# x turned over by TensorE, two tiles in every body, and the bias laid into the projection's bank by VectorE

## The reference

```python
qkv = (x @ w_qkv).reshape(b, n, 3, H, hd).transpose(2, 0, 3, 1, 4)
q, k, v = (qkv[0], qkv[1], qkv[2])
attn = jnp.einsum('bhnd,bhmd->bhnm', q, k) * scale
attn = jnp.where(attn_mask[None, None] == 0, -jnp.inf, attn)
attn = jax.nn.softmax(attn, axis=-1)
o = jnp.einsum('bhnm,bhmd->bhnd', attn, v).transpose(0, 2, 1, 3).reshape(b, n, d)
o = o @ w_proj + b_proj
mu = jnp.mean(o, axis=-1, keepdims=True)
var = jnp.mean(jnp.square(o - mu), axis=-1, keepdims=True)
ln = (o - mu) * jax.lax.rsqrt(var + LN_EPS) * ln_gamma + ln_beta
...
x = _layernorm(x + o + ln)
```

## Time and profile before

| | us |
|---|---|
| median of 3 executions | 3227.46 |
| lowest and highest | 3222.18 and 3236.81 |
| the profiled execution | 3231.68 |
| its span in the trace | 3229.8 |
| busy in it: PE, POOL, ACT, DVE | 2994.3, 2628.1, 2624.1, 2197.0 |

### The profile page before, as it was taken

The page is one execution under the profiler, slowest core; times in us unless marked ns, Lnnn a source line. Parts: engine busy times, 40 slices in busy tenths (PEclk is TensorE's granted clock), DMA queues, the critical chain, the costliest instruction groups (busy, mean ns, idle before and its releaser), DMA issues.

```text
span 3229.8 us, 119607 instructions
## 1 busy us (share of the span) xinstructions
PE 2994.3 (93%) x42112; PEld 1842.0 (57%) x42112; DVE 2197.0 (68%) x4243; ACT 2624.1 (81%) x3790; POOL 2628.1 (81%) x1610
## 2 busy tenths in 40 slices
PE   5889999899998999999999998999999899999995
PEld 2556556565565556656566565556556566565562
DVE  4546667677676767767677676767767677676775
ACT  5878878788787878878788787888888788787882
POOL 4768878788787878878798797888878788787884
PEclk9989999999999999999999999999999999999997
DMA  8999999999999999999999999999999999999994
GB/s 225 192 199 195 211 214 218 218 208 220 211 212 218 215 214 219 216 212 219 214 216 214 215 213 222 216 215 220 216 214 219 212 212 219 212 215 218 216 208 108
DMA packets 2320778, 682.49 MB, mean 211 GB/s; under 512 B 2268498, under 2 KB 2268498, under 8 KB 2320724
## 3 DMA queue, kind: packets, MB, share of 16 engines
q1 hardware_dynamic: 2266724, 581.58, 97.3%
q10 hardware_dynamic: 54000, 100.16, 9.7%
HBM read 77.60 MB, written 33.55 MB: 34 GB/s over the span
## 4 chain that ended last, share of the span: by engine, by line
POOL 54%; issue 29%; SPq 7%; PE 6%; DMA 2%; DVE 1%; POOLq 1%; ACT 1%; ACTq 0%; DVEq 0%
POOL p_split L742 42%; SPq L307 5%; POOL x_res L758 4%; POOL x_split L776 4%; POOL norm L766 2%; POOL norm L761 2%; PE scores_a L401 1%; PE side L360 1%; SPq L285 1%; DMA pt<-p_split 1%; PE side L347 1%; POOL shift L769 1%; POOLq L741 1%; PE proj L383 0%; PE pv_bank L422 0%
## 5 line engine op out<-in xcount | busy, mean ns | idle before, releaser
L742 POOL TENSOR_TENSOR p_split<-p,p_split 128x1024 f16<-128x1024 f32 x1024 | 2172.4, 2138 | 531.8 <-ACT p_split L507 526.0
L494 ACT ACTIVATE p<-p,row_min 128x1024 f32<-128x1024 f32 x1024 | 1167.9, 1142 | 91.9 <-DVE row_min L638 89.8
L507 ACT ACTIVATE p_split<-p 128x1024 f16<-128x1024 f32 x1024 | 1053.6, 1046 | 206.8 <-DMA pt<-p_split 205.9
L638 DVE CUSTOM_DVE_ANT_0 p<-scores_a,mask_q 128x1024 f32<-128x1024 f32 x512 | 626.9, 1224 | 502.3 <-PE scores_b L401 481.9
L422 PE MATMUL pv_bank<-v_both,pt 128*128 128x64 f16 x8192 | 840.0, 195 | 26.5 <-DMA pt<-p_split 24.6
L424 PE MATMUL pv_bank<-v_both,pt 128*128 128x64 f16 x8192 | 840.6, 195 | 0.0
L423 PE MATMUL pv_bank<-v_both,pt 128*128 128x64 f16 x8192 | 840.5, 195 | 0.0
L422 PEld LDWEIGHTS pv_bank<-v_both,pt 128*128 128x128 f16 x8192 | 747.9, 99 | 115.2 <-issue 39.6
L360 PE MATMUL side<-xt,w_hi 128*128 128x512 f16 x2048 | 683.2, 391 | 119.3 <-DMA xt<-x_split 114.3
L423 PEld LDWEIGHTS pv_bank<-v_both,pt 128*128 128x128 f16 x8192 | 736.9, 99 | 84.4 <-issue 6.0
L424 PEld LDWEIGHTS pv_bank<-v_both,pt 128*128 128x128 f16 x8192 | 737.4, 99 | 0.0
(11 more groups left out here) (80 smaller groups left out, 4261.3 us busy)
## 6 DMA issues: line engine op xcount, KB each, us to landing
x_in<-in_x ACTq DMA_DIRECT2D x63, 512.0 KB, 5.1
x_res<-in_x ACTq DMA_DIRECT2D x120, 256.0 KB, 3.3
out<-x_res ACTq DMA_DIRECT2D x120, 256.0 KB, 3.7
pt<-p_split SPq DMA_TRANSPOSE x1024, 4.8
pt<-in_adj SPq DMA_DIRECT2D x8, 512.0 KB, 9.7
ot<-in_L_gnn_w_qkv SPq DMA_DIRECT2D x4, 768.0 KB, 9.8
p<-in_x SPq DMA_DIRECT2D x4, 512.0 KB, 5.3
p<-in_x ACTq DMA_DIRECT2D x8, 256.0 KB, 8.5
```

What stands on the lines that cost most here:

```text
L494: nc.scalar.activation(p32[:, slot, :], p32[:, slot, :], ACT.Exp, bias=row_min[:, slot:slot + 1], scale=-1.0, accum_out=row_sum[:, head:he ...
L507: nc.scalar.activation(p_split[:, head % RING, HI, :], p32[:, head % RING, :], ACT.Copy).then_inc(hi_done, 1)
L638: nc.vector.tensor_tensor_reduce(out=p32[:, slot, :], in0=scores[ab][:, :], in1=mask_q[:, u, :], scale=-SCALE, scalar=3.0e38, op0=ALU.add, ...
L742: nc.gpsimd.tensor_tensor(p_split[:, slot, LO, :], p32[:, slot, :], p_split[:, slot, HI, :], ALU.subtract).then_inc(lo_done, 1)
```

## The change

- `xt` gets two halves, chosen by the parity of the batch. In each body g < 60 PE turns over the two tiles in `x_in` as float32, with 4 transposes each, as new side items X0 (after Q1) and X1 (in the middle of P0). ACT takes the hi part into `xt`, DVE the lo part. `x_split`, its splits on ACT and POOL, and SP's transposes of it are gone. The load of `x_in` now stands in slot 18 of the body before.
- The first batch's x is turned over by PE in the prologue, tile by tile, in turns with ACT and DVE.
- The bias matmul is gone. After "sum" DVE writes `bias_b` times 256 into `proj` (L591, `seed`), and the first matmul of the projection adds to it (`start=False`). In the prologue four matmuls of the identity (`bits_set`) mark the bank as written once. The rows in which the bias was prepared are gone.
- The tables `ORDER`, `COST`, `TAKE_ACT`, `TAKE_DVE` and `NORM_SLOTS` follow. Ten side items a body in place of eight. The loop ends at body 58, since bodies from 60 on have no X items.
- In the loop the half of `xt` depends on g, so its address is computed into registers for each matmul that reads it.

```diff
-ORDER = [("Q1", 0, 12), ("V0", 0, 48), ("V1", 0, 48), ("P0", 0, 4), ("O1", 0, 4), ("P0", 4, 13), ("Q0", 0, 12),
-         ("K0", 0, 12), ("K1", 0, 12), ("P1", 0, 9), ("O0", 0, 4), ("P1", 9, 13)]
+ORDER = [("Q1", 0, 12), ("X0", 0, 4), ("V0", 0, 48), ("V1", 0, 48), ("P0", 0, 4), ("O1", 0, 4), ("P0", 4, 7),
+         ("X1", 0, 4), ("P0", 7, 12), ("Q0", 0, 12), ("K0", 0, 12), ("K1", 0, 12), ("P1", 0, 9), ("O0", 0, 4),
+         ("P1", 9, 12)]
-LOOP = (PAIRS + 1, GROUPS - 1)
+LOOP = (PAIRS + 1, GROUPS - PAIRS - 1)
-        xt = sb("xt", [P, T, 2, KC, P], F16)
+        xt = sb("xt", [P, 2, T, 2, KC, P], F16)
...
-            for p in range(T // 2):
-                turn_x(FIRST_GROUP, p)
...
+                elif kind[0] == "X":
+                    if i == 0 and half == 0:
+                        wait_alone(pe, x_in_loaded, g * 16 + 16)
+                    mm = nc.tensor.transpose(bank[:, i * P:(i + 1) * P], x_in[:, half, i * P:(i + 1) * P], ident[:, :])
...
-                    mm = nc.tensor.matmul(bank[:, c * P:(c + 1) * P], xt[:, t, rows, k, :], w[:, k, OF_V, pair(g), :],
+                    mm = nc.tensor.matmul(bank[:, c * P:(c + 1) * P], xt[:, parity(batch(g)), t, rows, k, :],
+                                          w[:, k, OF_V, pair(g), :],
...
-                    if i == 0 and kind == NEXT_FIRST:
-                        wait_alone(pe, x_turned[0], batch(g + 1) * 32 + 32)
-                    if i == 0 and kind == "K1":
-                        wait_alone(pe, x_turned[1], batch(g + 1) * 32 + 32)
+                    if i == 0 and kind == NEXT_FIRST and active(g, "X1"):
+                        wait_alone(pe, side_dve, side_done(g, "X1"))
...
-                    nc.tensor.matmul(proj_bank(g, half), ones[:, :], bias_rows[:, :], start=False, stop=True).then_inc(proj_ready, 1)
...
-                wait_alone(act, x_lo_done, g + PAIRS)
-                source = x_pairs[(g + PAIRS) & (GROUPS - 1), :, :, :]
-                act.dma_start(x_in[:, :, :], source).then_inc(x_in_loaded, 16)
+                if not known(g) or g >= 0:
+                    wait_alone(act, side_ready, side_done(g, "X1"))
+                act.dma_start(x_in[:, :, :], x_pairs[g + (PAIRS + 1), :, :, :]).then_inc(x_in_loaded, 16)
...
+            def seed(g, i):
+
+                nc.vector.tensor_scalar(proj_bank(g, i), bias_b[:, :], WSCALE, None, ALU.mult).then_inc(seeds(g, i)[0], 1)
...
+                    wait_alone(dve, summed, n + 1)
+                    if not known(g) or g < GROUPS - 1:
+                        seed(g + i, 1 - i)
```

More of the change, by code:

```diff
@@ L233, in bodies @@
                 body(g)
[L235 to L241, removed]
         def heads(g, u, ab):
@@ L257, in proj_bank, with seeds @@
             return scores[0][:, 0:CH] if known(g) and g >= GROUPS and i == 1 else proj[:, :]
+        def seeds(g, i):
+            if known(g) and g >= GROUPS:
+                return (seeded[0], projected(GROUPS, 0) + (g - GROUPS + 1)) if i == 0 else (seeded[1], g - GROUPS + 1)
+            return seeded[0], projected(g, i) + 1
         def last_tile(g, i):
@@ L312, in body @@
                 for u in range(UNITS):
-                    for p in range(T // 2):
-                        if u == XT_UNIT[p] and not (known(g) and g == FIRST_GROUP):
-                            transposing(sp, g, lambda: turn_x(g, p))
                     ug, uk = unit_before(g, u, 1)
@@ L327, in _, with first_turn @@
             pe.wait_ge(ident_ready, 1)
+            def first_turn(t):
+                pe.wait_ge(x_first_loaded[t], 16)
+                wait(pe, x_first_lo, t - 1)
+                for k in range(KC):
+                    mm = nc.tensor.transpose(side[t % 2][:, k * P:(k + 1) * P], x_first[:, t, k * P:(k + 1) * P], ident[:, :])
+                mm.then_inc(x_first_turned, 1)
             def side_matmul(g, kind, i):
@@ L370, in project @@
                         pe.wait_ge(w_ready, 4 * KC)
[L371 to L376 removed]
+                    wait_alone(pe, *seeds(g, half))
                     if half == 0:
@@ L425, in times_v @@
                 mm.then_inc(pv_done, 1)
+            for t in range(T):
+                first_turn(t)
+            for k in range(KC):
+                mm = nc.tensor.matmul(proj[:, k * P:(k + 1) * P], ident[:, :], ident[:, :], start=(k == 0), stop=True,
+                                      skip_group_check=True)
+            mm.then_inc(bits_set, 1)
             def body(g):
@@ L481, in take @@
                                          bank[:, :].rearrange("p (t n) -> p t n", t=4), ACT.Copy).then_inc(side_act, 1)
+                elif kind[0] == "X":
+                    nc.scalar.activation(xt[:, parity(batch(g + PAIRS)), pair(g) * 2 + half, HI, :, :],
+                                         bank[:, :].rearrange("p (k n) -> p k n", k=KC), ACT.Copy).then_inc(side_act, 1)
                 elif kind[0] == "V":
@@ L770, in layer_norm @@
                                             ).then_inc(shifted, 1)
-            def split(g):
-                if known(g) and not 0 <= batch(g) < B - 1:
-                    return
-                wait_alone(pool, x_hi_done, g + PAIRS + 1)
-                nc.gpsimd.tensor_tensor(x_split[:, pair(g), :, LO, :], x_in[:, :, :], x_split[:, pair(g), :, HI, :],
-                                        ALU.subtract).then_inc(x_lo_done, 1)
-            for p in range(T // 2):
-                pool.wait_ge(x_hi_done, p + 1)
-                nc.gpsimd.tensor_tensor(x_split[:, p, :, LO, :], x_first[:, p, :, :], x_split[:, p, :, HI, :],
-                                        ALU.subtract).then_inc(x_lo_done, 1)
             def body(g):
```

150 lines of the change are left out of this document (66 added, 84 removed).

## The result

The changed kernel takes 3246.06 us (median of 6 runs, 3245.07 to 3251.43), the kernel before, run beside it, 3229.24. The ratio is 1.005, with a 95% interval of 1.0039 to 1.0061. 3124 us was forecast, within 3076 to 3178.

A forecast was written before the change was run, and what follows sets the result against it. PE was taken as the bound, with a DMA stall in every fourth body. Loop stretch -88, first bodies -10, last bodies -3, prologue -6.5, tail +4: -103.5 from 3231.7 profiled, 3128, less 4.2 for the median: 3124 us (3076 to 3178).

The forecast's parts named there:

- Part 1: x leaves SP's queue: Q0's and K1's DMA wait goes, long bodies become 46.2 us, 133 us off bodies 4 to 59.
- Part 5: Register steps for `xt`'s address at the loop's V matmuls: +0.7 us a body, between 0 and +2.8.
- Rival 3: Register steps stay fully on the path at V, and Q and K pay too: bodies 49.5 us, time 3248; chance 0.05.
- Part 4: Moved takes: O0's wait for K0's take goes, -0.28 us a body; V0 waits for Q1's take, +0.1.
- rival 5: Q0 waits for X1's takes as for the DMA, 3227 us; held unlikely, takes some 7 slots ahead; chance 0.02.
- Part 2: X0 and X1 on PE: eight float32 transposes at 0.115 us each, +0.92 us a body.
- rival 4: Each transpose occupies PE for its 285 ns: +82 us, time near 3206; chance 0.03.
- Part 3: Bias: two matmuls of 512 columns fewer a body on PE, -0.44 us; DVE takes over the seeds.
- The unrolled bodies: Bodies 60 to 63, without X: 4 x -0.72 = -3 us.
- The tail: Projections at the end also wait for the seed: +0.56 us for each of 7 or 8 tiles, +4 (0 to +5).
- Rival 2: Another wait in the body (DVE's order, `x_in` load or `pt` transposes): 47.8 to 48.6 us, time 3155 to 3200; chance 0.15.

The follow-up runs named there:

- b_steps: Kernel before with only V's read address of `xt` made to depend on the group, by an always-zero term: 3281.92 us, ratio 1.0157.
- a_fixed: Changed kernel with the half of `xt` fixed inside the loop, so no register steps for it and x stale: 3176.03 us, ratio 0.983.
- c_fixed: Changed kernel with c_order's order of side items and a_fixed's fixed half of `xt`: 3175.76 us, ratio 0.9829.
- c_order: Changed kernel with X0, X1 and O1 moved in the order of side items, their takes in slots 13, 14 and 16: 3241.76 us, ratio 1.0026.
- b_bias: Kernel before with the bias part alone: seeds by DVE, marking matmuls, no bias matmul: 3220.77 us, ratio 0.9966.
- b_unroll: Kernel before with the loop ended at body 58, so bodies 59 to 62 are unrolled: 3247.58 us, ratio 1.0055.

## Why the prediction was wrong

**Part 1 (the stall goes) was right.** No wait for x's DMA, equal bodies, clock 1.00. The gain of some 133 us was there. So the question is what cost as much.

**Part 5 (register steps) was mis-sized: +0.7 taken, 1.2 to 1.5 measured.** b_steps adds the steps alone and costs 1.46 us a body; a_fixed and c_fixed take them away and gain 1.31 and 1.16. I had both ends, 0 and 2.8, from the right rows, and chose nearer to zero with the argument that V's matmuls come in small groups between long ones. The table under b_steps shows what the argument missed: only behind the scores, two of seven times, is there cover; behind the short matmuls with `pt` the steps show. Rival 3's share for Q and K is out: they have 48 steps in the changed kernel's body where they had 26, and take 10.60 us against 10.59.

**Part 4 (moved takes) failed at two waits.** V0's wait for Q1's take was priced at +0.1, and its release was foreseen well (7.3 us into the body, measured 7.4). But a wait that ends just in time costs the sequencer its lead as well: the gap from X0 to V0 is 0.45 to 0.47 us where a transpose needs 0.11, so some 0.35, before any V matmul. And the first 11 V matmuls, now without lead, take 1.69 us (1.22 in a_fixed, 0.61 in the unrolled body 59, 0.62 behind the scores in b_steps). Where this wait is gone, in c_order (which moves X0, X1 and O1), V is 0.9 and X 0.5 lower: 1.4 us a body that were taken as 0.1, the larger of the two misses (0.8 without steps, from a_fixed to c_fixed). And rival 5 said that X1's takes were "some 7 slots" ahead of Q0. By `ORDER` and `COST` X1 ends in slot 15 and Q0 begins in slot 16: that was misread. From P0's last matmul to Q0 it is 0.46 us in the changed kernel and 0.70 to 0.79 in a_fixed (0.22 without a wait), so 0.24 and some 0.5 are its price. The take ends 0.7 us ahead of Q0's first matmul. O0's wait did go, as said.

**Part 2 held.** X costs 0.87 us in c_order and 1.06 in body 59, against 0.92; rival 4, with 2.3, is out. **Part 3 held nearly:** -0.37 us in the normal bodies of b_bias, on average, against -0.44. In the body of the changed kernel DVE's 36.5 busy us were cover enough, as said; c_order shows how little was to spare.

**The unrolled bodies were not seen at all.** The change moves four bodies out of the loop; I took -3 us for them by their matmuls, and they cost +6.2 (60 to 62). b_unroll has +6.1 in the kernel before, spread otherwise over the three; that the sums agree so well is in part luck. The row was there: body 4 of the kernel before, unrolled, took 48.19 us against 46.05 in the loop, and I wrote that down as start-up loss.

```profile
239.65:287.84 48.19, 47.10 (x661) 28.51 (x660) 30.23 (x58) 39.92 (x59) 39.28 (x22) 0.97 1.16 195
```

**The tail** was forecast at +4 us for the seeds, and that held: behind PE's last matmul with `pt` the kernel before takes 50.3 us, b_bias 54.5 and the changed kernel 54.6. The other 6.1 of the changed kernel's +10.5 lie ahead of it, in body 63, for which -0.7 was taken. There PE waits 25.1 us for transposes of `p_split`, before 20.5. Unrolling alone does not explain it (b_unroll, whose last body has the same form as before, has 1.5 more there); the rest stays open.

The sum of the misses: 54 x (48.98 - 47.2) = 96, 3 in bodies 4 to 6, 8 in 60 to 62, 7 behind, 2 ahead of body 4: 116 of the 122 us. Of the rest, 4 are what I took off for the median lying below the profiled execution; the changed kernel's lies 1 above. One side sum of part 1 was off too: at 1.73 to 1 the share of the 133 us in doubt is 0.42, or 56 us, not a third. It did not matter, since the whole surplus of the long bodies went. Rival 3 named the time (3248) and the side, but not the cause: it put all of +2.8 on the steps, where steps and waits just in time share it. Rival 2 had no part: PE waited 2.0 us in the whole run for a minimum, and at no time for the load of `x_in`.

## What to carry to other kernels

A double buffer that a loop addresses by parity makes each distinct address a register step on the reading engine. Count these against the length of the instructions just ahead of them: long ones give the sequencer time, short ones do not, and a wait that ends just in time takes away what it had. Where the removed stall comes once in four bodies, a cost of a quarter of it in each body cancels it: here 2.8 us against a mean stall of 9.5 / 4 = 2.4. And before fixing addresses by longer code, look whether the loop's code is fetched at all; here it was not (no row on q8 in the window of a loop body), and each way of making it longer cost more than the steps.

## What the runs showed of the hardware

- A step of PE's sequencer, 32 to 79 ns itself, comes every 0.12 us or so. 61 of them beside 96 matmuls that start 0.06 us apart cost 1.46 us of 47.5: nothing behind the scores, 0.2 to 0.5 us in each row behind short matmuls.
- A wait of PE that ended just in time cost 0.8 us a body without such steps behind it and 1.4 with them (V and X of a_fixed against c_fixed, of the changed kernel against c_order), where the wait itself is hardly seen.
- In the changed kernel's unrolled bodies 61 and 59 the DMA transposes of `p_split` held the DMA engines 14 and 18% longer for each MB than in its loop, while the instruction fetches themselves took 0.7 and 0.8% of these engines. In b_unroll the unrolled bodies without a stall took 46.1 to 51.1 us, where those of the loop take 46.1 to 46.8.
- A TensorE loop of eight bodies cost 8% of the time, and sixteen branches in each body, with V's code twice, 15%. They fetched 5.9 and 8.8 MB on q8, where the other kernels with a loop of one body fetched 0.6 to 1.0.
